# One layer of sparse attention and 64 experts: a reordered start, three shared-expert pairs behind the experts, three running sums kept to the end

## What is computed

```
x = x + attention(layernorm(x))      # 16 heads, window of 32, 16 global tokens
x = x + moe(layernorm(x))            # 64 experts, top 6 of each token, capacity 384
        + shared_swiglu(layernorm(x))
# attention: softmax over band and global keys, product with Wo, plus its residual
# moe: an expert's rows are gathered, silu(x wg) * (x wu) wd, weighted, added to the token's row
```

## Time and profile before

| what | us |
|---|---|
| median of 3 runs (lowest, highest) | 539.43 (537.42, 541.71) |
| the profiled execution | 542.53 |
| its span, first to last instruction | 540.7 |
| PE, DVE, ACT, POOL busy | 504.5, 363.2, 295.3, 334.2 |
| granted TensorE clock, mean | 0.956 |

### The profile page before, as it was taken

The page is one execution under the profiler, slowest core; times in us unless marked ns, Lnnn a source line. Parts: engine busy times, 40 slices in busy tenths (PEclk is TensorE's granted clock), DMA queues, the critical chain, the costliest instruction groups (busy, mean ns, idle before and its releaser), DMA issues.

```text
span 540.7 us, 13610 instructions
## 1 busy us (share of the span) xinstructions
PE 504.5 (93%) x4267; PEld 436.6 (81%) x4267; DVE 363.2 (67%) x1118; ACT 295.3 (55%) x899; POOL 334.2 (62%) x362
## 2 busy tenths in 40 slices
PE   7799999989999979899999999999999999999833
PEld 6698999878889969678888988888888888888722
DVE  3885788998998997675746556555565665556336
ACT  3697878997999973112243544554454454444300
POOL 4554246675666567870067768778888777776820
PEclk8997999997998988999999999999999999999976
DMA  8999999993222322227879999999999999987488
GB/s 284 386 357 364 404 403 381 351 375 119 89 96 103 97 84 96 94 107 239 246 173 234 251 254 247 257 252 275 247 261 285 265 270 242 257 190 164 51 234 263
DMA packets 72754, 126.35 MB, mean 234 GB/s; under 512 B 11329, under 2 KB 50049, under 8 KB 69601
## 3 DMA queue, kind: packets, MB, share of 16 engines
q1 hardware_dynamic: 46384, 65.57, 39.0%
q0 software_dynamic: 23616, 52.72, 36.2%
q10 hardware_dynamic: 2672, 7.09, 3.6%
HBM read 60.95 MB, written 62.32 MB: 228 GB/s over the span
## 4 chain that ended last, share of the span: by engine, by line
PE 52%; DMA 3%; issue 1%; DVE 1%; POOL 0%; SPq 0%; ACT 0%; POOLq 0%; DVEq 0%; ACTq 0%
PE PS L1012 17%; PE PS L1025 10%; PE PS L1016 8%; PE PS L1034 6%; PE PS L999 4%; PE PS L863 3%; PE PS L849 2%; DMA SMX<-acc_b 1%; DMA out<-YE,dest 1%; PE PS L838 1%; DMA acc_b<-YE,dest 1%; DVE X L1797 0%; POOL out L1967 0%; SPq L614 0%; ACT YE L1318 0%
## 5 line engine op out<-in xcount | busy, mean ns | idle before, releaser
L1952 POOL DMA_INDIRECT expert_rows<-XR,slot x96 | 95.4, 993 | 59.0 <-PE PS L683 33.1
L1967 POOL DMA_INDIRECT acc_b<-YE,dest x46 | 67.5, 1468 | 50.2 <-ACT YE L1318 39.2
L1318 ACT ACTIVATE YE<-PS,wsel 104x256 f32<-104x256 f32 (+14 forms) x128 | 49.9, 470 | 76.2 <-PE PS L1034 76.2
L1967 POOL DMA_INDIRECT out<-YE,dest x46 | 68.6, 1492 | 21.6 <-issue 10.1
L1742 DVE TENSOR_TENSOR PT<-SL,PS 128x216 f32<-128x216 f32 (+12 forms) x64 | 23.2, 362 | 80.9 <-ACT SL L1305 79.9
L1144 ACT ACTIVATE SMX<-SMX,smax 128x112 f32<-128x112 f32 x256 | 75.0, 387 | 2.5 <-DVE smax L1555 2.5
L1967 POOL DMA_INDIRECT acc_c<-YE,dest x36 | 53.0, 1472 | 14.3 <-issue 8.2
L1733 DVE COPY XET<-PS 128x432 f32<-128x432 f32 (+12 forms) x64 | 36.5, 572 | 12.9 <-PE PS L999 11.9
L1305 ACT ACTIVATE SL<-PS 128x216 f32<-128x216 f32 (+12 forms) x64 | 21.6, 337 | 41.4 <-PE PS L1012 40.8
L1541 DVE SCALAR_TENSOR_TENSOR SMX<-PS,mask 128x448 f32<-128x448 f32 x64 | 35.3, 613 | 6.3 <-PE PS L683 6.3
L750 PE MATMUL PS<-ident,SMX 128*112 128x128 f32 x240 | 35.7, 295 | 2.7 <-ACT SMX L1144 2.6
(11 more groups left out here) (242 smaller groups left out, 1165.0 us busy)
## 6 DMA issues: line engine op xcount, KB each, us to landing
expert_rows<-zero POOLq DMA_DIRECT2D x24, 1088.0 KB, 15.9
W<-in_w SPq DMA_DIRECT2D x24, 368.0 KB
XB<-in_w SPq DMA_DIRECT2D x15, 368.0 KB, 3.9
SMX<-in_w SPq DMA_DIRECT2D x15, 368.0 KB
XG<-expert_rows SPq DMA_DIRECT2D x18, 204.0 KB, 4.0
XG<-expert_rows SPq DMA_DIRECT2D x14, 238.0 KB, 4.5
W<-in_w SPq DMA_DIRECT2D x24, 128.0 KB
VS<-expert_rows SPq DMA_DIRECT2D x10, 238.0 KB, 4.7
```

The costliest lines, as they stand in the source:

```text
L1318: act.mul(YE[0:h, y_home(e), t, :], PS[0:h, 5 + t, e.odd * D:(e.odd + 1) * D], wsel[0:h, home(e), t:t + 1]).then_inc(y_ready, 1)
L1952: pool.indirect_dma_start(rows, bass.IndirectOffsetOnAxis(ap=slot[:, d2 % UN, k:k + 1], axis=0), XR[:, d2 % UN, :], None, bounds_check=EX ...
L1967: pool.indirect_dma_start(target, bass.IndirectOffsetOnAxis(ap=dest[0:h, home(e), t:t + 1], axis=0), YE[0:h, y_home(e), t, :], None, bound ...
```

## The change

- `NTL` goes from 4 to 6: four pairs run before the experts, three in `closing`. The gate product of pair 4 stands before the last down product of the experts.
- The sum array is `e % 3` to the end. `out` is read back when expert 61 has landed, `acc_c` when expert 62 has, `acc_b` when all have. DVE's order in `closing` is: product of pair 4, four quarters of `out`, product of pair 5, add of pair 4, four quarters of `acc_c`, product of pair 6, add of pair 5, three quarters of `acc_b`, add of pair 6, the last quarter.
- POOL's scatters don't wait for `s_done` (or, at the end, `pv_done`).
- Tile 1 is zeroed behind `root(0)`; `order_constants` moves to step 4; the sum arrays are zeroed in steps 9, 11 and 13; SP's wait for all zeroing moves from step 12 to behind the steps.
- `global_values` copies 2 of 8 in step 1 and 6 in step 2; the moments of blocks 4 to 15 move one piece later each; the norms of blocks 8 to 15 are split in two, and the residual norms of blocks 0 to 3 come before them.

```diff
-NTL = 4
+NTL = 6
-NORMED = (0, 1, NQ, 2 * NQ)
+NORMED = (0, 1, NQ, 2 * NQ, 3 * NQ)
...
         def target(e):
 
-            return e.off % 3 if e.i is not None or e.off <= LAST_C else e.off % 2
+            return e.off % 3
...
-            last = Step(LAST_C)
-            sp.wait_ge(y_stored[y_home(last)], last.turn(32, 32, YS))
-            sp.wait_ge(dn_done, LAST_C + 2)
-            sp.dma_start(XB[:, :, :], tokens(acc_c, 0, NT)).then_inc(c_back, 16)
-            sp.wait_ge(b_closed, 1)
+            for e, dst, back, src in ((EX - 3, XB, out_back, out), (EX - 2, XA, c_back, acc_c)):
+                last = Step(e)
+                sp.wait_ge(y_stored[y_home(last)], last.turn(32, 32, YS))
+                for k in range(4):
+                    sp.dma_start(dst[:, k * NQ:(k + 1) * NQ, :], tokens(src, k * NQ, NQ)).then_inc(back[k], 16)
+            sp.wait_ge(adds_closed, 1)
             for k in range(4):
-                sp.dma_start(XA[:, k * NQ:(k + 1) * NQ, :], tokens(acc_b, k * NQ, NQ)).then_inc(b_back[k], 16)
-            sp.wait_ge(out_closed, 1)
-            sp.wait_ge(summed, 4)
-            for k in range(4):
-                sp.dma_start(XB[:, k * NQ:(k + 1) * NQ, :], tokens(out, k * NQ, NQ)).then_inc(out_back[k], 16)
+                sp.wait_ge(summed, 1 + k)
+                sp.dma_start(XB[:, k * NQ:(k + 1) * NQ, :], tokens(acc_b, k * NQ, NQ)).then_inc(b_back[k], 16)
...
                     if e.odd:
+                        if half is graded_half and e.off == EX - 1:
+                            pair_gate(NPAIR)
                         down_two(e - 1)
...
             def closing():
 
-                pair_gate(NPAIR)
                 pair_up(NPAIR, pair_halves())
-                pair_gate(NPAIR + 1)
-                pair_down(NPAIR)
-                pair_up(NPAIR + 1, pair_halves())
-                pair_down(NPAIR + 1)
+                for p in range(NPAIR + 1, NPAIR + NTP):
+                    pair_gate(p)
+                    pair_down(p - 1)
+                    pair_up(p, pair_halves())
+                pair_down(NPAIR + NTP - 1)
...
                 if b1 == 0:
-                    global_values()
+                    global_values(0, 1)
+                if b1 == 1:
+                    global_values(1, UN)
                     moments(2)
-                if b1 == 1:
                     moments(3)
+                if b1 == 2:
                     moments(4)
-                if b1 == 2:
                     clear()
...
                 dve.wait_ge(d2_done, NPAIR)
-                dve.wait_ge(c_back, 16)
-                for k in range(4):
-                    add_quarter(k, XB, 1 + k)
                 tail_product(NPAIR)
                 for k in range(4):
+                    dve.wait_ge(out_back[k], 16)
+                    add_quarter(k, XB, 1 + k)
+                for p in range(NPAIR + 1, NPAIR + NTP):
+                    if p > NPAIR + 1:
+                        dve.wait_ge(d2_done, p - 1)
+                    tail_product(p)
+                    pair_add(p - 1)
+                    if p == NPAIR + 1:
+                        for k in range(4):
+                            dve.wait_ge(c_back[k], 16)
+                            add_quarter(k, XA, 5 + k)
+                for k in range(3):
                     dve.wait_ge(b_back[k], 16)
-                    add_quarter(k, XA, 5 + k)
-                tail_product(NPAIR + 1)
-                for k in range(3):
-                    dve.wait_ge(out_back[k], 16)
                     add_quarter(k, XB, 9 + k)
-                pair_add(NPAIR)
-                pair_add(NPAIR + 1)
+                pair_add(NPAIR + NTP - 1)
...
             norms(NQ, NQ)
-            norms(2 * NQ, 2 * NQ)
             residual_norms(0, NQ)
+            norms(2 * NQ, NQ)
+            norms(3 * NQ, NQ)
             residual_norms(NQ, NT - NQ)
-            for k in range(ZN):
-                zero_piece(pool, 1, k).then_inc(tile_zeroed[1], 16)
...
-                if s == LF + 3:
-                    order_constants()
+                if c == 0:
+                    for k in range(ZN):
+                        zero_piece(pool, 1, k).then_inc(tile_zeroed[1], 16)
...
-                    if live(b1 + 1):
-
-                        pool.wait_ge(s_done, 2 * (b1 + 2))
-                    elif b1 >= NT:
-
-                        pool.wait_ge(pv_done, RG * NT)
...
+                if c == 1:
+                    order_constants()
```

More of the change, by code:

```diff
@@ L61 @@
 LAG = 4
-LAST_C = 53
 FC = 3
 NL = 2
-NTL = 4
+NTL = 6
 NPAIR = (NT - NL - NTL) // 2
@@ L326, in build @@
         y_stored = sem2("y_stored", YS)
-        b_closed, out_closed = sem("b_closed"), sem("out_closed")
-        c_back, b_back, out_back = sem("c_back"), sem2("b_back", 4), sem2("out_back", 4)
+        adds_closed = sem("adds_closed")
+        c_back, b_back, out_back = sem2("c_back", 4), sem2("b_back", 4), sem2("out_back", 4)
         summed, out_stored = sem("summed"), sem("out_stored")
@@ L532, in step @@
                         weights(j, j)
[L533 to L536, removed]
             steps(step)
+            for t in range(TPE):
+                sp.wait_ge(tile_zeroed[t], 16 * ZN)
+            sp.wait_ge(sums_ready, 16 * 3)
             sp.wait_ge(pt_done, RG * NT)
@@ L812, in step @@
                     pe.wait_ge(vw_loaded[b2 % UN], vw_all(b2))
-                    if b2 == 0:
-                        pe.wait_ge(glob_values, 1)
+                    if b2 < 2:
+                        pe.wait_ge(glob_values, b2 + 1)
                     for n in range(RG):
@@ L858, in pair_down @@
                 else:
-                    pe.wait_ge(sh_add, NL + 2 * min(p, NPAIR))
+                    pe.wait_ge(sh_add, NL + 2 * max(min(p, NPAIR), p - 1))
                 hid, ps = pair_home(p)
@@ L1173, in step @@
                 a, b1, b2, c, d1, d2, e1 = (s - k for k in (0, LB, LP, LC, LD, LE, LE))
-                if s in (LF + 1, LF + 2, LF + 3):
+                if s in (LF + 3, LF + 5, LF + 7):
                     na = T // P * D // 4
-                    sums = (acc_b, out, acc_c)[s - LF - 1]
+                    sums = (acc_b, out, acc_c)[(s - LF - 3) // 2]
                     act.wait_ge(zero_ready, 1)
@@ L1411, in _, with global_values @@
             dve.memset(zero[:, :], 0.0).then_inc(zero_ready, 1)
-            def global_values():
+            def global_values(first, end):
                 dve.wait_ge(glob_done, 2)
-                for t in range(UN):
+                for t in range(first, end):
                     for k in range(NB):
@@ L1799, in closing @@
                 dve.wait_ge(d2_done, NPAIR)
[L1800 to L1802 removed]
                 tail_product(NPAIR)
                 for k in range(4):
+                    dve.wait_ge(out_back[k], 16)
[10 more added lines that the diff above has]
+                for k in range(3):
                     dve.wait_ge(b_back[k], 16)
[L1806 to L1809 removed]
                     add_quarter(k, XB, 9 + k)
[L1811 to L1812 removed]
+                pair_add(NPAIR + NTP - 1)
                 dve.wait_ge(sh_add, NT)
[L1814 removed]
+                dve.wait_ge(b_back[3], 16)
                 add_quarter(3, XB, 12)
@@ L1974, in main @@
                 if not e.first(3):
-                    before = same_target(e)
+                    before = e - 3
                     hold(pool, y_stored[y_home(before)], before.turn(32, 32, YS))
@@ L2004, in _ @@
                 landed(3)
-            last_b = Step(EX - 2)
-            pool.wait_ge(y_stored[y_home(last_b)], last_b.turn(32, 32, YS))
-            pool.sem_inc(b_closed, 1)
             landed(2)
-            pool.sem_inc(out_closed, 1)
+            pool.sem_inc(adds_closed, 1)
 def kernel(**inputs):
```

2 lines of the change are left out of this document (1 added, 1 removed).

## The result

The changed kernel takes 535.44 us (median of 20 runs, 531.95 to 537.50) and the kernel before 539.08 in the same measurement (20 runs, 535.87 to 541.71): a ratio of 0.9936, 95% interval 0.9915 to 0.9957. That is -3.6 us where I had forecast -8.0. The profiled execution took 535.43 us with a span of 533.6; that of before had taken 542.53 with 540.7.

The account below looks back on a forecast made before the run. PE bounds the kernel until 500 us, something else the end. Start -0.9 and 0, step 9 -3.5, scatters -0.4 and 0, hand-over -3.5, end +0.3 sum to -8.0: from 539.43 to 531.4, range 527.0 to 538.5.

Parts of the forecast that it names:

- The end: Closing stretch behind the experts: earlier reads of `out` against 7.1 us more DVE work; +0.3, between -0.9 and +3.5.
- DVE is busy throughout: Closing: after the fourth quarter of `out` is added at 520.9, DVE works without a break to 535.9; -0.6 if PE keeps up.
- halfway value: Closing: PE may come back slow after waiting for product 5, making product 6 2.0 later; halfway gives +0.3.
- the end is one engine's queue: Rival, closing: DVE serves three arrays in fixed order, last landings slow, PE goes slow; +3.5 instead of +0.3, chance 0.15.
- The start: First attention steps: split copies and moved moments -0.9, zero pieces behind `root(0)` 0.
- copies: Start: with two copies in front instead of eight, PE's first transposes wait less; -0.9, between 0 and -2.6.
- first root: Start: `root(0)` still starts near 45.3, its wait only changing cause; 0, between -1.5 and +0.8.
- Step 9: Attention step 9: moving the memset of `YE` to step 4 removes DVE's 1.84 us operation; -3.5, between -1.7 and -4.3.
- Scatters: Freed scatters: -0.4 in attention's last steps, where POOL is the chain; otherwise 0, between -2 and +2.
- the rivals of the stalls and of the lock: Scatters stall DVE: +16.7, 548.1, chance 0.06; each `rows` waits for the rest of a scatter: +5, 536.4, chance 0.06.
- The third rival: The memset in step 4 meets DVE's `rows(1)`, or the clock falls elsewhere; step 9's gain vanishes: 534.9, chance 0.12.
- Hand-over: Start of the experts: one pair leaves PE's path, so the hidden layer begins sooner; -3.5, between -2.1 and -4.6.

Follow-up runs that it names:

- a_order: The changed kernel with DVE's products of pairs 5 and 6 ahead of quarter 2 of `out` and of `acc_c`: 533.73 us, ratio 0.9911.
- b_again: The kernel before, unchanged, timed once more as the null: 537.06 us, ratio 0.9972.
- b_end: The kernel before with only the change's end (three pairs behind the experts, three sum arrays): 537.38 us, ratio 0.9988.
- b_front: The changed kernel without its end, so two pairs behind the experts and two sum arrays at the end: 534.83 us, ratio 0.9923.
- b_const: The kernel before with `order_constants` moved from step 9 to step 4, nothing else: 536.59 us, ratio 0.9957.
- a_again: The changed kernel, unchanged, timed once more: 535.51 us, ratio 0.9945.
- a_moments: The changed kernel with the start's moments, norms and copies in the order of before, tile 1's zero pieces still behind `root(0)`: 531.19 us, ratio 0.9873.
- m_order: a_moments plus the earlier products of a_order at the end: 526.57 us, ratio 0.9785.
- a_const: The changed kernel with the constants back in step 9: 534.68 us, ratio 0.9908.
- m_split: m_order with two of the eight copies of the global values in front and six a step later: 528.60 us, ratio 0.9815.
- a_scatter: The changed kernel with GpSimd's waits for PE's next score products back in front of the scatters: 537.31 us, ratio 0.9981.
- a_early: The changed kernel with tile 1's zero pieces issued between the norms of blocks 8 to 11 and 12 to 15: 535.43 us, ratio 0.9938.
- w_again: a_win, unchanged, timed once more: 530.36 us, ratio 0.9846.
- a_win: The changed kernel with the earlier zero pieces of a_early and the earlier products of a_order: 530.07 us, ratio 0.9830.

## Why the prediction was wrong

- **The end: the term that failed.** I had +0.3, from "DVE is busy throughout" and a halfway value between full and lower clock. Measured from the hidden layer to the end: 287.02 on the mean of eight kernels with the new end and the change's order of products, 284.05 on that of five with the old end: +3.0. The adds ended as I had said (last one at 504.51, 257.8 behind the hidden layer; forecast 257.1), and so did SP's first read (254.4; forecast 253.7). What failed are two steps. "Then DVE is busy throughout": quarters of `out` were ready 4.5, 6.1, 8.5 and 10.5 us behind their issue, not 4.8 to 9.7, and the product that PE stood for, behind the fourth, came about 1 us later than forecast. And the halfway value for PE's clock: in all eight profiles PE stood 4.6 to 5.5 us for that product, its down took 4.8 to 5.5 us instead of 2.75, and DVE waited 1.1 to 1.7 for its `up`. That is the rival "the end is one engine's queue", priced at +3.5 and given 0.15. a_order shows it by removal: 2.7 of the 3.0 go in its profile, 2.2 on the mean of the seven kernels with its edit, and in all seven the down takes 2.86.
- **The start.** Forecast: copies -0.9, first root 0. Root(0) came at 45.99 (forecast 45.3), and its wait did change its cause. But PE's wait of 2.60 became one of 2.38 for `xnT`, and the first to fourth scores took 29.0 at best and 32.0 in the profiled execution: no -0.9. The step with the split copies fell from 12.95 (mean of seven) to 12.19 (mean of thirteen), -0.8, so that term was sized well in the trace. What failed is the price of the moved moments, which I had at 0 with a bound of +0.8: the next step is 1.5 longer in every kernel that has them. The two together are +0.7, 1.6 over the forecast. Root(0) costs what it cost before (the step behind the fourth scores takes 13.6 on the mean of the five kernels with its old order, 13.5 on that of the twelve with the new one), as forecast. But the pieces' move could have given 3 us there: with the old moments and norms the step is 10.5. I had added these edits to 0 and had not looked at each alone. The pieces' move by itself was not run.
- **Step 9** (-3.5): the stretch from the 7th to the 11th scores went from 48.5 (mean of before, b_again and b_end) to 45.1 (mean of the change's two profiles, b_front and a_order), -3.4. In the trace the size is right, the cause half: the free scatters alone do it. In the time b_const, the memset's move alone, gave 0.5 to 2.2 us and not 3.5; how much of the difference is noise stays open. Two of these four profiles lost 1.7 to 3.5 us in the step ahead, where late zeros hold root(5). In eight profiles with free scatters block 2's scatters wait for a zero and DVE for none: where root(5) starts at most 0.6 us behind the ninth scores the step takes 10.9 to 11.4 (a_again, a_order, a_moments, m_order), where it starts 1.1 to 1.6 behind them 12.5 to 14.5 (the change, b_front, a_const, m_split). I had priced the zero pieces at nothing ("tile 1 has a whole step before its first scatter") and had not looked at tile 2's, which stand behind them in the queue.
- **Scatters** (-0.4): about -1.8, by a_scatter and the two stretches. No `rows` at 0.8 us in most steps; the rivals of the stalls and of the lock have nothing for them. The third rival came true in half: the memset in step 4 does meet `rows` of block 1 (0.95 us instead of 0.41), but no engine waits for it.
- **Hand-over** (-3.5): 14.49 to 10.96, -3.53. PE stood once and not twice as forecast, 2.5 us for DVE's product, and it never waited for rows: they had landed when its down was done, in the change, where that came back slow (4.51 us), and in a_early, where it took 2.83. The size hangs on the clock: ten of the fifteen profiles with this end have 10.8 to 11.0, three (a_early, a_scatter, w_again), where PE kept its clock, 9.4 to 9.5, so -5.0, and two (a_order, a_win) 12.2. That -3.5, a middle value, was met so closely is in part luck.
- **From one execution to the median.** I took the terms off an execution of 542.53, above all 20 in the measurement, and carried them over whole ("the terms are in every execution"). Its twin b_again had a span 3.4 us shorter: 1.4 from the 4th to the 7th scores, 0.8 in the stretch with step 9, 0.9 from the 11th to the 16th, 0.7 at the end. Part of the stall was that execution's own.

In sum: end 2.7 over, start 1.6 over, scatters 1.4 under make 2.9 of the 4.4 us by which I was off. Step 9, 1.3 or more over by b_const's time, would fill the rest, but it is no larger than what the null shows (1.5), and so is not shown. The halves measured -3.9 and -1.4 against 538.7, and the whole -3.6 and, once more, -3.1.

## What to carry to other kernels

Price each edit of a group alone: here the start's edits were priced together at about nothing, and taking some of them back gave 4 us; and two edits shared one gain that had been booked to one of them. In a closing stretch where one engine serves landings and another engine's operands in a fixed order, put the operand that the other engine stands for ahead of the landing that isn't there yet. A transfer that is moved later in a full queue moves all that is behind it: look for the last consumer, not the first.

## What the runs showed of the hardware

- A vector operation of 6 elements that had started before GpSimd's memset ended only with it: 113.20 + 1.93 = 115.13 and 114.14 + 0.95 = 115.09 in b_end; the same in the kernel before. When it started, GpSimd was in the instruction in front, a scatter (112.62 to 113.59); that scatter, the root and the memset followed each other within 0.02 us. In the changed kernel the memset's place in step 4 met the writing of a block (0.95 instead of 0.41 us), which nobody waited for.
- Short pauses cost more in clock than in waiting: in the changed kernel PE stood 0.59 and 0.62 us ahead of the fourth block's scores, and the window from 44 to 54 us ran at a mean granted clock of 0.66; without them, in a_moments, at 1.00.
- Two profiled executions of one kernel differ by 3.4 us of 540, with mean granted clocks of 0.956 and 0.963.
- With GpSimd's queue full of zero pieces, the wait from issue to landing grew from 4.6 us (issued at 46.5) to 28.5 (issued at 55.7), and landings did not come in the order of issue: in the changed kernel the last piece, issued at 81.3, landed at 99.6, and scatters issued from 83.7 on landed from 97.4.
